# Spreading a row of target terms over the partitions: from a product with 128 equal weight columns to a turn of one column read 128 times

## The reference, cut to what matters

```
h = (node_feats @ W.T + b).reshape(B, N, 4, 32)
l_src = einsum('bihc,hc->bih', h, a[:, :32])
l_dst = einsum('bjhc,hc->bjh', h, a[:, 32:])
logits = leaky_relu(l_src[:, :, None, :] + l_dst[:, None, :, :], 0.2)
logits = where(adj == 1, logits, -9e15)
probs = softmax(logits, axis=2)
out = einsum('bijh,bjhc->bihc', probs, h)
```

## Time and profile before

| | |
|---|---|
| median of 3 runs | 1065.88 us (1065.15 to 1066.37) |
| the profiled execution's own time | 1066.04 us |
| its span in the trace | 1063.9 us |
| TensorE busy (matmuls) | 954.6 us, 90% |
| VectorE busy | 892.3 us, 84% |
| ScalarE busy | 864.0 us, 81% |
| GpSimd busy | 132.6 us, 12% |
| mean granted TensorE clock, share of full speed | 0.967 |
| DMA | 52.32 MB, mean 49 GB/s |

### The profile page before, as it was taken

One profiled execution on the slowest core, in us unless ns is written; L12 is line 12 of the kernel. 1 busy time (PEld: TensorE's weight loads), 2 busy tenths in 40 slices (PEclk: granted clock), 3 DMA queues, 4 the chain that ended last, 5 costly groups with the idle time before them and its releaser, 6 DMA issues.

```text
span 1063.9 us, 16086 instructions
## 1 busy us (share of the span) xinstructions
PE 954.6 (90%) x5024; PEld 609.6 (57%) x5024; DVE 892.3 (84%) x2710; ACT 864.0 (81%) x1860; POOL 132.6 (12%) x170
## 2 busy tenths in 40 slices
PE   4588998999989899999989899998989999998866
PEld 3455565666566566656556566656656665655443
DVE  5296989899898979899897989989897989979543
ACT  3367888979888897988888897988889798887742
POOL 1102011010202011020201201020201101010000
PEclk8558999999999999999999999999999999999989
DMA  2401204021210403121220402121030302111000
GB/s 72 109 1 39 72 11 109 11 61 52 68 51 14 106 11 77 44 60 51 56 64 10 110 11 60 60 61 51 15 105 11 79 31 61 50 40 51 1 11 10
DMA packets 42477, 52.32 MB, mean 49 GB/s; under 512 B 1296, under 2 KB 25872, under 8 KB 42384
## 3 DMA queue, kind: packets, MB, share of 16 engines
q0 software_dynamic: 16896, 25.17, 10.7%
q1 hardware_dynamic: 17040, 21.83, 6.5%
q10 hardware_dynamic: 8448, 4.20, 1.3%
HBM read 55.39 MB, written 4.19 MB: 56 GB/s over the span
## 4 chain that ended last, share of the span: by engine, by line
PE 52%; DVE 28%; ACT 10%; issue 6%; POOL 3%; DMA 0%; DVEq 0%; SPq 0%; ACTq 0%; POOLq 0%
PE l_bank L948 7%; DVE probs L642 6%; PE a_bank L981 6%; PE x_bank L1040 4%; PE a_bank L948 3%; PE h_bank L1102 3%; ACT hn L394 3%; PE r_bank L1102 3%; PE r_bank L1105 3%; DVE sess L843 3%; DVE sess L836 3%; PE h_bank L1105 3%; PE n_bank L1105 3%; DVE probs L663 3%; POOL rstd L363 2%
## 5 line engine op out<-in xcount | busy, mean ns | idle before, releaser
L663 DVE SCALAR_TENSOR_TENSOR probs<-spread,s_lift,probs 128x512 f32<-128x512 f32 x320 | 237.4, 747 | 4.0 <-DVE rmax L642 0.5
L642 DVE CUSTOM_DVE_ANT_0 probs<-spread,mask 128x512 f32<-128x512 f32 x320 | 211.8, 684 | 2.4 <-ACT spread L450 2.3
L363 POOL TENSOR_TENSOR rstd<-var_eps,power 128x4 f32<-128x4 f32 x64 | 88.0, 1375 | 882.5 <-DVE var_eps L636 603.0
L460 ACT ACTIVATE probs<-probs,shift_p 128x512 f32<-128x512 f32 x256 | 185.7, 725 | 5.7 <-DVE shift_p L659 5.7
L468 ACT ACTIVATE pT<-l_bank 128x512 f32<-128x512 f32 x256 | 151.8, 600 | 46.5 <-PE l_bank L948 46.3
L948 PEld LDWEIGHTS l_bank<-ident,probs 128*128 128x128 f32 x1024 | 124.3, 144 | 73.8 <-issue 46.0
L948 PE MATMUL l_bank<-ident,probs 128*128 128x128 f32 x1024 | 150.5, 278 | 6.1 <-ACT probs L460 5.1
L394 ACT ACTIVATE hn<-x,shift,rstd 128x128 f32<-128x128 f32 x192 | 80.5, 492 | 26.1 <-POOL shift L365 26.0
L1005 PE MATMUL l_bank<-hT,dst_rep 128*128 128x512 f32 x128 | 73.6, 658 | 12.1 <-ACT pT L468 8.5
L870 DVE SCALAR_TENSOR_TENSOR hid_n<-r_t,hid_n 128x512 f32<-128x512 f32 x48 | 33.1, 689 | 57.8 <-ACT r_t L518 57.8
L981 PE MATMUL a_bank<-values,pT 128*128 128x128 f32 x512 | 65.7, 286 | 0.7 <-ACT pT L428 0.7
(11 more groups left out here) (175 smaller groups left out, 1956.5 us busy)
## 6 DMA issues: line engine op xcount, KB each, us to landing
adjt_i<-in_adj_t SPq DMA_DIRECT2D x16, 1024.0 KB, 5.2
edges<-in_adj POOLq DMA_DIRECT2D x16, 1024.0 KB, 5.9
adj_h<-in_adj POOLq DMA_DIRECT2D x16, 512.0 KB, 7.7
xin<-in_x SPq DMA_DIRECT2D x16, 256.0 KB, 2.9
out<-out_sb ACTq DMA_DIRECT2D x16, 256.0 KB, 3.8
weights_sb<-in_weights SPq DMA_DIRECT2D x1, 840.0 KB, 4.7
```

Source lines behind the costliest of these rows:

```text
L363: g.tensor_tensor(rstd[n][:], var_eps[n][:], power[:], op=ALU.pow).then_inc(pool_step[n], 1)
L460: s.activation(row, row, ACT.Exp, bias=shift_p[:, head, c:c + 1], accum_out=den[:, head, c:c + 1]).then_inc(probs_ready, 1)
L642: return v.tensor_tensor_reduce(out=row, in0=spread_row, in1=mask, scale=1.0 / LIFT, scalar=-3e38, op0=ALU.subtract, op1=ALU.max, accum_ou ...
L663: v.scalar_tensor_tensor(row, spread_row, source, row, ALU.min, ALU.subtract, reverse1=True).then_inc(ready, 1)
```

## The change

The target terms of all four heads become four more columns of `values1_w`, beside the source terms, and both are scaled there: sources by -0.8, targets by 0.8. One VectorE addition per bank (128 x 272) now takes values, sources and targets out together, with a bias row that holds the heads' constants for the sources and zero for the targets; the two small operations of L741 are gone, and `s1_lift` with them. The spreads of heads 2 to 4 no longer are a matmul: TensorE turns, for each of the four chunks, a 128 x 128 operand which is one column of `values1`, read 128 times (a step of 0). Head 1's spread stays a matmul, since it is due before the values are. Waits, semaphores and counts stay as they were. In the constants, three of five `dst_rep` blocks are no longer made, and two small operations come in.

```diff
--- before.py
+++ after.py
@@ -163,7 +163,10 @@
     HD = D // H1
     HEADS = 1 + H1
     UNITS = H1 * C
-    COUNT_AT = 2 * (D + H1)
+
+    COLS1 = D + 2 * H1
+    SOURCE1, TARGET1 = D, D + H1
+    COUNT_AT = 2 * COLS1
     KINDS = 4
     LAYERS = 3
     REST = KINDS - 1
@@ -196,14 +199,13 @@
         b1_rep = sb("b1_rep", [P, P])
         src_w = sb("src_w", [P, HEADS])
         dst_w = sb("dst_w", [P, HEADS])
-        dst_rep = sb("dst_rep", [P, HEADS, P])
-        head_const = sb("head_const", [P, H1])
+        dst_rep = sb("dst_rep", [P, 2, P])
         head_parts = sb("head_parts", [P, 2, H1])
-        b1_rows = sb("b1_rows", [P, D])
+        b1_rows = sb("b1_rows", [P, COLS1])
 
         b2_left, b2_part = sb("b2_left", [P, D]), sb("b2_part", [P, D], bf16)
         b2_parts, ones_h = sb("b2_parts", [P, C, D], bf16), sb("ones_h", [P, P], bf16)
-        values1_w = sb("values1_w", [P, D + H1])
+        values1_w = sb("values1_w", [P, COLS1])
         gi_w = sb("gi_w", [P, LAYERS, 3 * D])
         gate_b = sb("gate_b", [P, 3])
         half_bhn = sb("half_bhn", [P, 1])
@@ -229,8 +231,8 @@
         counted = sb("counted", [P, C, N], bf16)
         count = sb("count", [P, 1])
         other_kinds = sb("other_kinds", [P, 2], i32)
-        values0, values1 = sb("values0", [P, C, D]), sb("values1", [P, C, D])
-        s1_lift = sb("s1_lift", [P, HEADS, C])
+        values0, values1 = sb("values0", [P, C, D]), sb("values1", [P, C, COLS1])
+        s10_lift = sb("s10_lift", [P, C])
         rmax, shift_p, den = sb("rmax", [P, HEADS, C]), sb("shift_p", [P, HEADS, C]), sb("den", [P, HEADS, C])
         above, below, empty = ([sb(f"{m}{n}", [P, C]) for n in range(2)] for m in ("above", "below", "empty"))
         rden = sb("rden", [P, HEADS, C])
@@ -595,18 +597,21 @@
                 v.tensor_copy(src_w[:, 1:HEADS], l_bank1[:, 2:2 + H1])
                 v.tensor_copy(dst_w[:, 1:HEADS], l_bank1[:, 2 + H1:2 + 2 * H1])
                 cw.own(v.tensor_copy(head_parts[:, :, :].rearrange("p a h -> p (a h)"), l_bank1[:, 16:16 + 2 * H1]))
-                for h in range(HEADS):
+                for h in range(2):
                     last = v.tensor_scalar(dst_rep[:, h, :], ones[:], dst_w[:, h:h + 1], LIFT, ALU.mult, ALU.mult)
                 cw.own(last)
 
             def more_constants():
-                cw.own(v.tensor_tensor(head_const[:], head_parts[:, 0, :], head_parts[:, 1, :], ALU.add))
-                cw.own(v.tensor_scalar(head_const[:], head_const[:], LIFT, None, ALU.mult))
+                source_const = b1_rows[:, SOURCE1:SOURCE1 + H1]
+                v.memset(b1_rows[:, TARGET1:TARGET1 + H1], 0.0)
+                cw.own(v.tensor_tensor(source_const, head_parts[:, 0, :], head_parts[:, 1, :], ALU.add))
+                cw.own(v.tensor_scalar(source_const, source_const, -LIFT, None, ALU.mult))
                 dve.wait_ge(pe_w, 2)
-                v.tensor_copy(b1_rows[:], l_bank0[:, 0:D])
+                v.tensor_copy(b1_rows[:, 0:D], l_bank0[:, 0:D])
                 v.tensor_copy(b2_left[:], l_bank0[:, D:2 * D])
                 v.tensor_copy(values1_w[:, 0:D], w1t_sb)
-                v.tensor_copy(values1_w[:, D:D + H1], src_w[:, 1:HEADS])
+                v.tensor_scalar(values1_w[:, SOURCE1:SOURCE1 + H1], src_w[:, 1:HEADS], -LIFT, None, ALU.mult)
+                v.tensor_scalar(values1_w[:, TARGET1:TARGET1 + H1], dst_w[:, 1:HEADS], LIFT, None, ALU.mult)
                 cw.own(v.memset(b2_parts[:, :, :], 0.0))
                 for n in range(3):
                     row = slice(32 * n, 32 * n + 1)
@@ -642,12 +647,15 @@
                 return v.tensor_tensor_reduce(out=row, in0=spread_row, in1=mask, scale=1.0 / LIFT, scalar=-3e38,
                                               op0=ALU.subtract, op1=ALU.max, accum_out=top)
 
+            def sources(head):
+                return values1[:, :, SOURCE1 + head - 1] if head else s10_lift[:, :]
+
             def shift_part(p, head, part):
                 k = min(head, 1)
                 heads, nth = (1, 1) if head == 0 else (H1, head)
                 if part == "top":
                     dve.wait_ge(max_ready[k], p.count(heads, nth))
-                    v.scalar_tensor_tensor(above[k][:, :], rmax[:, head, :], -1.0, s1_lift[:, head, :], ALU.mult, ALU.add)
+                    v.scalar_tensor_tensor(above[k][:, :], rmax[:, head, :], -1.0, sources(head), ALU.mult, ALU.add)
                     v.tensor_scalar(empty[k][:, :], rmax[:, head, :], -2.0, -MASK, ALU.mult,
                                     ALU.add).then_inc(shift_step[k], 1)
                 elif part == "below":
@@ -679,7 +687,7 @@
                                     ALU.mult).then_inc(mask0_ready, 1)
                 elif step == "src0":
                     dve.wait_ge(src0_ready, p.count(1, 1))
-                    v.tensor_scalar(s1_lift[:, 0, :], a_bank[:, 0:C], -LIFT, None, ALU.mult).then_inc(s10_copied, 1)
+                    v.tensor_scalar(s10_lift[:, :], a_bank[:, 0:C], -LIFT, None, ALU.mult).then_inc(s10_copied, 1)
                 elif step[0] == "m" and step[1:].isdigit():
                     c = int(step[1])
                     if c == 0:
@@ -697,7 +705,7 @@
                     if c == 0:
                         dve.wait_ge(s10_copied, p.count(1, 1))
                         dve.wait_ge(max_ready[0], p.count(1, 1))
-                    logits(probs0[:, c, :], spread0[:, :], s1_lift[:, 0, c:c + 1], logits0_ready)
+                    logits(probs0[:, c, :], spread0[:, :], s10_lift[:, c:c + 1], logits0_ready)
                 elif step == "den0":
                     dve.wait_ge(probs0_ready, p.count(C, C))
                     v.tensor_scalar(alive[:, :], rmax[:, 0, :], -MASK / 2, None, ALU.is_gt)
@@ -734,14 +742,9 @@
                     if prev.exists():
                         dve.wait_ge(l1_done, prev.count(1, 1))
                     for half in range(2):
-                        both = l_banks[half][:, 0:2 * (D + H1)].rearrange("p (c k) -> p c k", c=2)
-                        pair = slice(2 * half, 2 * half + 2)
-                        v.tensor_tensor(values1[:, pair, :], both[:, :, 0:D],
-                                        b1_rows[:, :].unsqueeze(1).to_broadcast([P, 2, D]), ALU.add)
-                        last = v.scalar_tensor_tensor(s1_lift[:, 1:HEADS, pair],
-                                                      both[:, :, D:D + H1].rearrange("p c h -> p h c"), -LIFT,
-                                                      head_const[:, :].unsqueeze(2).to_broadcast([P, H1, 2]),
-                                                      ALU.mult, ALU.subtract)
+                        both = l_banks[half][:, 0:2 * COLS1].rearrange("p (c k) -> p c k", c=2)
+                        last = v.tensor_tensor(values1[:, 2 * half:2 * half + 2, :], both,
+                                               b1_rows[:, :].unsqueeze(1).to_broadcast([P, 2, COLS1]), ALU.add)
                     last.then_inc(val1_copied, 1)
                     v.tensor_scalar(other_kinds[:, par:par + 1], l_bank0[:, COUNT_AT:COUNT_AT + 1], P * PLAIN, None,
                                     ALU.not_equal).then_inc(others_ready, 1)
@@ -769,7 +772,8 @@
                         dve.wait_ge(val1_copied, p.count(1, 1))
                     if c == 0:
                         dve.wait_ge(max_ready[1], p.count(H1, head))
-                    logits(probs[:, head % 2, c, :], spread[:, head % 2, :], s1_lift[:, head, c:c + 1], logits_ready)
+                    source = values1[:, c, SOURCE1 + head - 1:SOURCE1 + head]
+                    logits(probs[:, head % 2, c, :], spread[:, head % 2, :], source, logits_ready)
 
             def kinds_of(p, k):
                 if k > 1:
@@ -943,6 +947,11 @@
                 if ready is not None:
                     last.then_inc(ready, 1)
 
+            def spread_column(dst, columns, k, ready):
+                for c in range(C):
+                    last = t.transpose(dst[:, c * P:(c + 1) * P], columns[:, c, k:k + 1].to_broadcast([P, P]), ident[:])
+                last.then_inc(ready, 1)
+
             def turn(dst, row, ready):
                 for j in range(C):
                     last = t.transpose(dst[:, j * P:(j + 1) * P], row[:, j * P:(j + 1) * P], ident[:])
@@ -1002,15 +1011,17 @@
                         pe.wait_ge(val1_copied, p.count(1, 1))
                     else:
                         pe.wait_ge(pT_copied, p.count(UNITS, (0, 0, 0, 2, 5)[head]))
-                    t.matmul(l_banks[head % 2][:, :], dst_rep[:, head, :], hT[1][:, :], start=True,
-                             stop=True).then_inc(dst_ready, 1)
+                    if head == 1:
+                        t.matmul(l_bank1[:, :], dst_rep[:, 1, :], hT[1][:, :], start=True, stop=True).then_inc(dst_ready, 1)
+                    else:
+                        spread_column(l_banks[head % 2], values1, TARGET1 + head - 1, dst_ready)
                 elif step == "values1":
```

(4 more changed lines are left out.)

## The result

| | before | changed |
|---|---|---|
| median | 1065.64 us (6 runs: five from 1065.06 to 1066.37, one of 2443.47) | 1071.01 us (1069.31 to 1072.8, 6 runs) |
| ratio, 95% interval | | 1.0056 [1.0045, 1.0066] |
| profiled execution, its span | 1066.04, 1063.9 us | 1072.0, 1069.9 us |
| TensorE, VectorE, ScalarE busy | 954.6, 892.3, 864.0 us | 939.1, 890.4, 864.3 us |
| mean granted clock | 0.967 | 0.956 |

The one run of 2443.47 us is not explained; the ratio goes by the others. The forecast was 3.0 us faster; it came out 5.4 us slower. The page of the changed kernel answers to the earlier trace rows: TensorE was busy for 15.5 us less (some 20 were forecast; work that falls into a half clock counts twice as long), the chain's shares are nearly the same, and the time is longer.

What follows compares the result with a forecast made beforehand. The steady path was taken to run on VectorE, then TensorE, with the turned spreads off it. 1.8 + 1.5 - 0.1 - 0.2 = 3.0 us off 1065.9 gave 1062.9 us, range for 8 in 10 1057.5 to 1067.0.

Steps and rivals of the forecast that it cites:

- Where the path runs: Steady cycle: VectorE's half, then TensorE's; dst2 to dst4 lie in VectorE's half, so TensorE's saving there becomes idling.
- VectorE, 1.8 us: Values and sources on VectorE: 0.11 us less in each of 16 graphs, all on the path, 1.8 us.
- The turn at 0.44 us: Spreads of heads 2 to 4: four turns of a repeated column take 0.44 us, where a spread took 0.86.
- 1.5 us from the first graphs, nothing in steady state: TensorE's spreads: 0.8 us in graph 0, 0.3 in graph 1, 0.4 at two later single ones; otherwise nothing.
- The clock: Around dst4 of graph 0 and dst2 of graph 1: less matmul work may delay a clock rise, 0.2 us lost.
- The sign that I had named for being wrong: The prediction is wrong if windows after 150 us show a granted clock under 1.00.
- a rival with 10%: Steady cycles: clock falls behind turned dst4, 1.5 to 2 us each; 1075.5 us for seven falls, 1068.3 for three; 10%.
- one stretch of turns and idling that kept its clock: TensorE from 88.18 to 92.70 us: only turns and idling, clock 1.00 from 90 to 92; cited against the clock rival.

Runs made afterwards that it cites:

- values-only: Changed kernel with all four spreads as matmuls again, keeping one addition per bank for values, sources and targets: 1065.97 us, ratio 0.9996 to the kernel before.
- the tail held: One addition per bank, all spreads matmuls, plus products in the last graph's idle stretches: 1059.85 us; the kernel before with the same products: 1061.77 us.
- half products: Changed kernel plus a 256-column float32 product ahead of the turns of heads 3 and 4: 1064.46 us, ratio 0.9998 to the kernel before.
- Turns made twice: Changed kernel with the four turns of heads 3 and 4 made twice: 1064.20 us, ratio 0.9998 to the kernel before.

## Why the prediction was wrong, step by step

- *Where the path runs*: right. The three spreads lie in VectorE's half, and what TensorE saved on `dst3` and `dst4` turned into idling (0.84 to 1.31 us behind `dst4`).
- *VectorE, 1.8 us*: right in size. 0.12 us less in the rows, 0.10 us per cycle in the values-only trace, 1.9 us with the tail held, which by itself isn't clear of the intervals.
- *The turn at 0.44 us*: right. The turns stand 0.11 us apart (464.80 to 465.23 for four).
- *1.5 us from the first graphs, nothing in steady state*: VectorE's wait for `dst3` of graph 0 fell from 2.26 us to 1.29 us, as said. What it gave in the end I can't confirm: the first `x2` came 1.7 us earlier, but 1.15 us earlier with values only as well, and 0.6 us later with half products, as the clock moves there; two executions with the same values-only start differ by 1.5 us at this point (96.67 and 95.19). The second was short by 0.09 us per cycle on average, from `dst2`, some 1.3 us in all, in five of the 14 cycles. How it reaches the path I did not settle.
- *The clock*: this term failed. I put 0.2 us for it, looked at graphs 0 and 1 only, where the clock was moving already, and left the steady cycles to a rival with 10%. The sign that I had named for being wrong, a clock under 1.00 after 150 us, came. The saving that does nothing for the path made TensorE idle longer ahead of the place where the path moves to it. That costs 8 x 1.2 us in the profiled execution, against some 3 us of gains.
- *The rival that came true* was priced at 1.5 to 2 us a fall (measured 1.2) and placed well (seven falls of eight at the first sum). It missed layer 2's sum behind `dst3`. What misled me was one stretch of turns and idling that kept its clock: it showed that a stretch can pass, not that it passes 14 times. In the changed kernel, too, about half of the stretches passed, with the same instructions.
- The Trainium skill's rule, that a transpose does not count as activity in the same way and that the full clock does not engage for it ("TensorE: Matmul & The Clock Gate", Part 4: PE-mode transpose), pointed to the right danger, but not to the right cause. Turns made twice hold the clock as half products do (1064.20 and 1064.46 us, one set), so for these float32 turns the measurement decides against it. It was the shorter work, not its kind.

Open stays why of alike stretches some lose the clock and others don't. Their phase differs from execution to execution (the changed kernel's runs have mean clocks of 0.954 to 0.959), but nothing here varied it on purpose. Open too is whether the shorter work counts or the longer wait that it leaves (1.31 us ahead of L940 in place of 0.84): each experiment moved both together. A single wait of that length is not enough, since with double turns TensorE waits 1.36 us ahead of L945 (at 482.15 us) and keeps its clock.

## What to carry to other kernels

A saving on an engine that waits there anyway isn't free of effect: on TensorE it made the idle stretches longer here, and the next stretch on the path may pay with half the clock. So look at what TensorE does in the last microseconds before the path moves to it, in every cycle, and price a fall by the instructions that follow (here 2.2 us of sums became 3.4). Where TensorE waits off the path, useless work can cost nothing and be worth more than the change: here 7 us at the start and the tail (1064.09 to 1056.82 us for the kernel before), against 2 us for the change itself.

## What the hardware showed that I had not expected

- Doubled turns and products of equal length hold the clock alike (above).
- Executions of one kernel differ by 7 us (values only: 1061.09 to 1068.32 us), with the higher mean granted clock in the shorter ones (0.976 to 0.964), and by 9.9 us with a product ahead of head 4's turns. Holding the tail as well left values only 3.7 us apart (7 runs), but the kernel before 5.1 us (12 runs), so that it narrows the spread in general isn't shown.
- The same instructions with the same waits may or may not bring a fall. In the last graph the wait of 5.6 us has one in the kernel before and in values only alike; behind two waits of 2.9 us the kernel before has none, and values only has two.
